# Graph attention on one core: where two bursts of scores, the block transfers of the last pairs and one transpose stand in the closing section

## What is computed

```python
q = heads(x @ Wq + bq); k = heads(x @ Wk + bk); v = heads(x @ Wv + bv)
scores = einsum('bhqd,bhkd->bhqk', q, k) / sqrt(32)
scores = where(adj == 0, -inf, scores)
out = einsum('bhqk,bhkd->bhqd', softmax(scores), v)
y = x + out @ Wo + bo
result = (y - mean(y)) / sqrt(var(y) + 1e-5)
```

## Time and profile before

| | us |
|---|---|
| median of three runs | 813.85 |
| lowest, highest | 813.26, 815.09 |
| the profiled execution, its own time | 814.74 |
| span of the profiled execution | 811.2 |

### The profile page before, as it was taken

The page is one execution under the profiler, slowest core; times in us unless marked ns, Lnnn a source line. Parts: engine busy times, 40 slices in busy tenths (PEclk is TensorE's granted clock), DMA queues, the critical chain, the costliest instruction groups (busy, mean ns, idle before and its releaser), DMA issues.

```text
span 811.2 us, 26937 instructions
## 1 busy us (share of the span) xinstructions
PE 801.9 (99%) x11772; PEld 679.3 (84%) x11772; DVE 641.0 (79%) x998; ACT 268.3 (33%) x346; POOL 550.4 (68%) x442
## 2 busy tenths in 40 slices
PE   9999999999999999999999999999999999999997
PEld 7778888888888888888888888888888888888876
DVE  5778778887778887788877788877888777876895
ACT  6533333222333223332223332233322333323223
POOL 1786677766686666786767767667866668655672
PEclk9999999999999999999999999999999999999999
DMA  8333544344452534534445343454435345234342
GB/s 322 132 80 113 166 121 140 104 142 141 118 172 75 173 119 118 177 92 139 118 119 176 112 138 112 138 158 118 152 91 163 120 118 177 71 108 117 95 107 104
DMA packets 64437, 106.62 MB, mean 131 GB/s; under 512 B 11712, under 2 KB 27584, under 8 KB 62144
## 3 DMA queue, kind: packets, MB, share of 16 engines
q1 hardware_dynamic: 51840, 87.59, 34.4%
q10 hardware_dynamic: 12480, 17.32, 8.1%
HBM read 54.53 MB, written 16.78 MB: 88 GB/s over the span
## 4 chain that ended last, share of the span: by engine, by line
PE 95%; POOL 2%; ACT 1%; DVE 1%; DMA 0%; issue 0%; POOLq 0%
PE ring L363 15%; PE ring L365 15%; PE ring L364 15%; PE ring L512 7%; PE ring L513 7%; PE ring L516 7%; PE psum_s L463 6%; PE psum_s L433 6%; PE ring L454 6%; PE psum_s L465 6%; PE psum_s L467 6%; POOL soft L1138 1%; POOL t_lo L1121 1%; DMA qt<-in_wq 0%; PE ring L383 0%; POOL s_lo L1126 0%
## 5 line engine op out<-in xcount | busy, mean ns | idle before, releaser
L1138 POOL TENSOR_TENSOR soft<-soft,top 128x1024 f32<-128x1024 f32 x62 | 123.3, 1989 | 20.9 <-DVE top L921 20.9
L229 POOL TENSOR_TENSOR soft<-soft,inverse 128x1024 f32<-128x1024 f32 x62 | 118.8, 1917 | 26.0 <-DVE inverse L928 25.9
L925 DVE TENSOR_REDUCE total<-soft 128x16 f32<-128x1024 f32 x62 | 75.3, 1214 | 50.6 <-ACT soft L703 50.6
L703 ACT ACTIVATE soft<-soft 128x1024 f32<-128x1024 f32 x62 | 65.9, 1063 | 115.9 <-POOL soft L1138 115.9
L363 PE MATMUL ring<-x_hi,wk_hi 128*128 128x512 f32 x256 | 103.1, 403 | 0.0
L365 PE MATMUL ring<-x_hi,wk_lo 128*128 128x512 f32 x256 | 99.9, 390 | 0.0
L364 PE MATMUL ring<-x_lo,wk_hi 128*128 128x512 f32 x256 | 99.7, 389 | 0.0
L512 PE MATMUL ring<-wo_hi,ot_hi 128*128 128x512 f32 x252 | 99.0, 393 | 0.0
L513 PE MATMUL ring<-wo_lo,ot_hi 128*128 128x512 f32 x252 | 98.9, 392 | 0.0
L363 PE MATMUL ring<-x_hi,wq_hi 128*128 128x512 f32 x248 | 96.8, 390 | 1.7 <-ACT qt L690 1.7
L738 ACT CAST s_hi<-v 128x1024 fp32r<-128x1024 f32 x27 | 28.3, 1048 | 211.3 <-DVE v L874 211.3
(11 more groups left out here) (124 smaller groups left out, 1876.5 us busy)
## 6 DMA issues: line engine op xcount, KB each, us to landing
pt<-soft SPq DMA_DIRECT2D x248, 64.0 KB, 2.5
x_raw<-in_xt SPq DMA_DIRECT2D x15, 1024.0 KB, 7.0
row<-in_x SPq DMA_DIRECT2D x60, 256.0 KB, 2.6
out_rows<-row SPq DMA_DIRECT2D x60, 256.0 KB, 2.8
pt<-soft ACTq DMA_DIRECT2D x232, 64.0 KB, 2.4
v<-in_xt SPq DMA_DIRECT2D x27, 512.0 KB, 5.0
adj<-in_adj SPq DMA_DIRECT2D x16, 128.0 KB, 2.7
kt<-in_wk SPq DMA_DIRECT2D x4, 256.0 KB, 5.7
```

The costliest lines, as they stand in the source:

```text
L229: ops.tensor_tensor(soft_of(c), soft_of(c), on_keys(inverse[:, c % 2, :]), ALU.mult).then_inc(normed, 1)
L925: nc.vector.tensor_reduce(total[:, c % 2, :], by_row_head(soft_of(c)), AX_XY, ALU.add).then_inc(summed, 1)
L1138: nc.gpsimd.tensor_tensor(soft_of(c), soft_of(c), on_keys(top[:, c % 2, :]), ALU.subtract).then_inc(centred, 1)
```

## The change

On PE, `score(T-6)`, `score(T-5)` come after `project_out(T-10)` and not before it; `score(T-4)`, `score(T-3)` come before `project_out(T-9)` and not after it. SP and ACT wait for the scores of T-3 before they start the blocks of T-6, and for those of T-1 before the blocks of T-4. The blocks of T-4 and T-3 are started by both queues. On DVE `add_row(T-10)` stands ahead of the masks of T-6 and T-5, `mask(T-4)` ahead of `add_row(T-9)`, `sum_up(T-4)` ahead of `split_ot`, and `read_v(T-5)` and `turn(T-3)` ahead of `add_y(T-8)`. On ACT `exp(T-4)` comes ahead of `read_ot`.

```diff
-SHARED = (*range(TILES - 4), TILES - 2, TILES - 1)
+SHARED = range(TILES)
...
             load_row(T - 6)
+            sp.wait_ge(scored, T - 2)
             place(T - 6)
             place(T - 5)
             store(T - 9)
             load_row(T - 5)
+            sp.wait_ge(scored, T)
             for c in range(T - 4, T):
                 place(c)
...
+            pe.wait_ge(ot_lo_done, PAIRS - 4)
+            project_out(T - 10)
             score(T - 6)
             score(T - 5)
-            pe.wait_ge(ot_lo_done, PAIRS - 4)
-            project_out(T - 10)
...
             project_v(T - 7)
-            project_out(T - 9)
 
             score(T - 4)
             score(T - 3)
+            project_out(T - 9)
...
             read_k(T - 1)
+            act.wait_ge(scored, T - 2)
             place(T - 6)
             place(T - 5)
             norm_by_act(T - 9)
 
+            exp(T - 4)
             read_ot(PAIRS - 4)
-            exp(T - 4)
             exp(T - 3)
+            act.wait_ge(scored, T)
+            place(T - 4)
+            place(T - 3)
             exp(T - 2)
...
+            add_row(T - 10)
             mask(T - 6)
             mask(T - 5)
-            add_row(T - 10)
...
+            mask(T - 4)
             add_row(T - 9)
-
-            mask(T - 4)
             mask(T - 3)
+            sum_up(T - 4)
             split_ot(PAIRS - 4)
-            sum_up(T - 4)
             read_v(T - 6)
             sum_up(T - 3)
             turn(T - 4)
+            read_v(T - 5)
+            turn(T - 3)
             add_y(T - 8)
-            read_v(T - 5)
 
             mask(T - 2)
             add_y(T - 7)
-            turn(T - 3)
```

## The result

The changed kernel takes 822.49 us (median of six runs, 820.77 to 823.89) against 813.73 us of six runs before on the same chip (812.75 to 815.09): a ratio of 1.0105, 95% interval 1.0095 to 1.0116. It is 8.8 us slower. Forecast were 5.6 us more and a range to 821.8, so the direction was right and the time lies outside.

What follows compares the result with a forecast made beforehand. PE, busy for 99% of the span, was taken to bound the kernel. Waits of 7.30 us less gains of 1.67 gave net +5.6, so 813.85 + 5.6 = 819.5 us, range 817.6 to 821.8.

Steps and rivals of the forecast that it cites:

- The four waits: New waits of PE at `project_k(T-1)`, `project_v(T-7)`, `mix(T-8)` and `project_out(T-8)`: 0.35 + 1.27 + 1.97 + 3.71 = 7.30 us.
- The first two: PE waits 0.35 us for `read_v` at `project_k(T-1)` and 1.27 us for `read_q` at `project_v(T-7)`.
- The third: PE waits 1.97 us before `mix(T-8)`, as `mask(T-4)` and `add_row(T-9)` wait for the blocks of T-6 to land.
- DVE's idle time ahead of the mask: DVE stands idle for 4 to 5 us before the mask of T-4, released by a transfer.
- The fourth: PE waits 3.71 us for `split_ot` at `project_out(T-8)`.
- The dear bursts of scores: Two score bursts on PE, at 737.86 and 756.32, recorded with 1.99 us; away from transfers each gives back 0.40.
- part 3: Blocks of T-4 wait for the scores of T-1, on two queues: no wait of PE, and 0.87 us gained.
- The 0.87 goes: The mixing burst at 775.48, 2.28 us instead of 1.41, loses its extra 0.87, since block starting is just over.
- The rival of the dear bursts: Bursts stay dear, perhaps through PE's supply of small instructions: +0.8 to +1.7 us, so 820.3 to 821.2; chance 0.14.
- The free ACT time: Eight more block starts on ACT, 5.3 us, end at 781.8, before the input of `exp(T-2)` at about 782.3: free.
- The clock: Rival: the clock falls in the 3.7 us wait at `project_out(T-8)`, 2 us lost, time 821.6; chance 0.14.

Runs made afterwards that it cites:

- e7: The kernel before plus only the wait of SP and ACT for the scores of T-3 ahead of the blocks of T-6: 821.11 us, ratio 1.0082.
- e4: The kernel before with 130 waits that do nothing put into PE's program: 812.25 us, ratio 0.9971.
- e1: The kernel before with the new order of PE alone (the two swaps): 817.00 us, ratio 1.0033.
- e12: The changed kernel without the wait for the scores of T-3 and with 130 waits in PE's program: 820.70 us, ratio 1.0071.
- e3: The changed kernel with 130 waits that do nothing put into PE's program: 819.83 us, ratio 1.0069.
- e5: The changed kernel with 40 more waits of PE in the loop, a single run: 820.74 us.
- e11: The kernel before with 130 waits in PE's program and the blocks of T-4 and T-3 on two queues: 813.88 us, ratio 0.9998.
- e8: The kernel before with the blocks of T-4 and T-3 on two queues and no wait for scores: 814.85 us, ratio 1.0010.
- e6: The changed kernel with the blocks of T-4 and T-3 started by SP alone, still behind the scores of T-1: 821.07 us, ratio 1.0081.

## Why the prediction was right in direction and wrong in size

*The four waits* were right. Forecast 0.35 + 1.27 + 1.97 + 3.71; recorded 0.16, 0.97, 2.51 and 2.17. The first two are recorded shorter, since part of them is hidden in the modelled ends of matmuls: from start to start the two groups ahead take 3.04 and 3.99 where 2.72 is clean, 1.6 us together as forecast. The third is the landing: I counted 2.2 us from the start of a block's issue, and the chain has 2.24 us from its end (759.98), behind 0.69 of issue, so 2.97 in all. Of this step's bounds, 2.0 to 3.0, the upper end came. DVE's idle time ahead of the mask, forecast as 4 to 5 us, is 5.30. Adjusted for the 0.9 of the start, `project_out(T-8)` begins 0.6 later than worked out. The fourth is shorter by what the clock took out of it.

*The dear bursts of scores* were right: 0.40 + 0.40 came back. The burst of T-4 goes with the busy share of the DMA engines while it runs: clean (1.52) up to a share of 0.65 (0.39 in the changed kernel, 0.04 in e7, 0.65 in e4) and dear from 0.79 on (1.93 at 0.82 before, 2.12 at 0.79 in e1, 1.98 at 0.95 in e12). The mixing burst of T-8 went the same way, from 1.48 at 0.52 before to 2.11 at 0.82 in e7. But the share is not all of it: the burst of T-6 occupies 1.91 at 0.64 before and 1.56 at 0.67 in e4, whose only difference is the 130 places.

*The failed step* is in part 3: "The 0.87 goes: at 781.97 starting is just over". Starting was all but over indeed (ACT's ends at 783.64, the burst begins at 783.59), and the loss did not go. I took the transfers' nearness for the whole cause, compared with one clean burst at 788.87 that has other instructions ahead of it, and passed over the row at 777.53, whose 0.60 us without a semaphore was in the trace of before. The gap is bound to the length of PE's program ahead of it (e3, e4 and e5 against seven kernels with the old length). What the burst loses went from 0.87 to 1.99 us: the gain was 0.8, not 1.67, and 1.1 us of new loss came on top. Why the packet, and with it the gap, comes later in the changed kernel and in e1 stays open. e3, with the burst at 1.76 us, lies 5.6 us over before, which is the forecast; in part that is luck, since its interval runs from 4.2 to 7.0 us and its profile is 6.3 us longer than that of before in the closing section. The rival of the dear bursts named the supply of instructions, and was the nearest to the truth, but its price of 0.8 to 1.7 took the loss before as the largest it could be.

*The free ACT time* in part 3 was right for the changed kernel, by a hair: the starts end at 783.64 and the centred input of `exp(T-2)` is ready at 783.70. e3, which has no gap to hide a delay, shows no wait for the split there either. In the order of before, `turn(T-3)`, whose result the blocks of T-3 carry, ends only at 774.37 (e11): ACT's starts last 8.20 us instead of 5.62, past the centred input of `exp(T-2)`, and a wait of 1.1 us follows (e8 and e11).

*The clock* was put down as a rival behind the fourth wait. It did fall, and after a shorter wait (2.5 us), where the next wait swallowed it. In e6 and e5, with the same order of work, it fell once more behind the second wait, of 1.80 us, and that cost 1.6 us. It is likely to be a part of the spread of 3.1 us over six runs of the changed kernel: the two longest (823.22 and 823.89) have the lowest mean granted clock, 0.994, and the shortest (820.77) has 1.000, though so has one of 822.44. The Trainium skill, "TensorE: Matmul & The Clock Gate", Part 1, says of the return to the full clock that its point varies from run to run; whether the fall's does too no trace here can show, as there is one profile of the changed kernel.

*What stays open:* why bursts in some kernels take up to 0.7 us longer with neither a gap nor a fall of the granted clock (the 1.99 of the earlier trace rows, 1.85 in e5, 2.21 in e11). The blocks have to do with it, and for the burst of T-6 the position in the program, but no run separates the two. And what holds the q8 packet back in the changed kernel and in e1.

## What to carry to other kernels

Where one engine is busy all the time, a wait added on a transfer queue is a wait added on everything that needs the buffer which the transfer frees: follow it to the busy engine before it is written, and count the landing from the end of the issue. Look for gaps with no semaphore at the same instruction count in several kernels, and try to shift the program by some instructions (40 and 130 were tried here) before work is rearranged. A wait of 2 to 4 us on PE had a second price here, the slower clock behind it, nearly as large as the wait in one case.

## What the runs showed of the hardware that was not expected

A burst of small matmuls stood still for 0.53 to 1.72 us at a fixed place in the program, in all seven profiles with the same length of program ahead of it, and went on 2.3 to 3.0 us behind a packet of the instruction queue. That it had outrun the supply of its own instructions fits this, and is not seen directly. A shift of the program by 130 places, and by 40 in a single run, took the gap away, and 130 useless instructions made the kernel before 0.2 to 0.3% faster (ratios 0.9971 and 0.9979). And the clock fell to its lower level (0.50 of full granted) behind waits of 1.8 to 4.4 us in a kernel that is otherwise busy throughout, at places that differ between kernels with the same order of work.
